# Behind the last head group: SiLU in one ACT instruction, the second output product by channel halves, normalisation pair by pair

## What is computed

```python
h = layer_norm(y, sb_norm_w, sb_norm_b) * (1.0 + scale) + shift
h = jax.nn.silu(h) @ out_w + out_b
return x + h
```

## Time and profile before

| what | value |
|---|---|
| median of 3 runs | 515.12 us (514.90 to 515.36) |
| time of the profiled execution | 515.57 us |
| its span, first to last instruction | 513.8 us |
| mean granted TensorE clock | 0.993 of full |
| PE busy | 504.3 us, 98% of the span |
| DVE / ACT / POOL busy | 412.0 / 344.6 / 220.4 us |

### The profile page before, as it was taken

One profiled execution on the slowest core, in us unless ns is written; L12 is line 12 of the kernel. 1 busy time (PEld: TensorE's weight loads), 2 busy tenths in 40 slices (PEclk: granted clock), 3 DMA queues, 4 the chain that ended last, 5 costly groups with the idle time before them and its releaser, 6 DMA issues.

```text
span 513.8 us, 9864 instructions
## 1 busy us (share of the span) xinstructions
PE 504.3 (98%) x3346; PEld 195.1 (38%) x3346; DVE 412.0 (80%) x1059; ACT 344.6 (67%) x677; POOL 220.4 (43%) x253
## 2 busy tenths in 40 slices
PE   9999899999999999999999999999999999999987
PEld 5563423333443244333433334332433333332234
DVE  4876897998897688966898688967899999999226
ACT  1453367776767675777768576777778778777961
POOL 3039749999143420832226430643672045005401
PEclk8899999999999999999999999999999999999999
DMA  6983232242214133110331133210331112211011
GB/s 240 349 273 102 80 93 79 64 143 83 76 53 125 41 124 125 41 43 17 113 122 43 43 97 110 68 49 11 124 124 43 43 43 87 81 44 43 2 41 42
DMA packets 43034, 45.26 MB, mean 88 GB/s; under 512 B 4436, under 2 KB 41572, under 8 KB 42600
## 3 DMA queue, kind: packets, MB, share of 16 engines
q1 hardware_dynamic: 42696, 42.79, 26.6%
q10 hardware_dynamic: 288, 1.84, 0.9%
HBM read 25.46 MB, written 18.87 MB: 86 GB/s over the span
## 4 chain that ended last, share of the span: by engine, by line
PE 75%; DVE 11%; issue 2%; POOL 2%; ACT 2%; POOLq 0%; DVEq 0%; ACTq 0%
PE bank L549 19%; PE bank L532 12%; PE bank L523 10%; PE bank L595 9%; PE bank L512 9%; DVE masked L862 7%; PE bank L623 4%; PE bank L606 4%; PE bank L564 2%; PE bank L584 2%; ACT probs L715 1%; DVE row_max L865 1%; PE bank L557 1%; PE bank L631 1%; POOL XN L836 1%
## 5 line engine op out<-in xcount | busy, mean ns | idle before, releaser
L715 ACT ACTIVATE probs<-bank 128x512 f32<-128x512 f32 x512 | 272.4, 600 | 82.0 <-PE bank L523 81.2
L865 DVE TENSOR_REDUCE row_max<-bank 128x1 f32<-128x512 f32 x256 | 162.9, 684 | 29.5 <-PE bank L532 27.9
L532 PE MATMUL bank<-k_s,q_s 64*128 64x512 f16 x512 | 182.7, 382 | 1.8 <-DVE row_max L865 1.2
L862 DVE CUSTOM_DVE_ANT_0 masked<-bank,mask_bias 128x512 bf16<-128x512 f32 x256 | 162.9, 687 | 13.0 <-PE bank L532 12.0
L512 PE MATMUL bank<-q_s,k_s 64*128 64x512 f16 x512 | 151.8, 381 | 0.9 <-ACT v_aug L783 0.5
L523 PE MATMUL bank<-shift,kx 64*128 64x512 f16 x512 | 148.6, 376 | 0.0
L549 PE MATMUL bank<-probs,v_aug 128*17 128x512 f32 x1024 | 135.4, 598 | 0.7 <-ACT probs L715 0.7
L532 PEld LDWEIGHTS bank<-k_s,q_s 64*128 64x128 f16 x512 | 46.1, 93 | 151.8 <-DVE row_max L862 67.1
L595 PE MATMUL bank<-xT,wqkv 128*128 128x512 f32 x128 | 61.7, 612 | 0.4 <-ACT xT L746 0.3
L523 PEld LDWEIGHTS bank<-shift,kx 64*128 64x128 f16 x512 | 46.8, 95 | 32.0
L512 PEld LDWEIGHTS bank<-q_s,k_s 64*128 64x128 f16 x512 | 31.6, 94 | 13.4 <-ACT probs L715 8.0
(11 more groups left out here) (111 smaller groups left out, 512.3 us busy)
## 6 DMA issues: line engine op xcount, KB each, us to landing
q_parts<-parts SPq DMA_DIRECT2D x64, 128.0 KB
k_parts<-parts SPq DMA_DIRECT2D x64, 128.0 KB
q_s<-q_parts SPq DMA_DIRECT2D x32, 256.0 KB, 2.7
k_s<-k_parts SPq DMA_DIRECT2D x32, 256.0 KB, 3.0
X<-in_x SPq DMA_DIRECT2D x4, 512.0 KB, 7.3
y<-X SPq DMA_DIRECT2D x7, 256.0 KB, 2.2
wc<-in_w_cond ACTq DMA_DIRECT2D x1, 1024.0 KB, 5.1
tables<-in_tables SPq DMA_DIRECT2D x4, 256.0 KB, 7.1
```

The lines of the kernel that those rows point to most:

```text
L532: nc.tensor.matmul(bank, m.q_s[slot][rows, i, queries], m.k_s[slot][rows, i, :], start=True, stop=True).then_inc(q.d_made, 1)
L715: act.activation(m.probs[k][:, h, :], bank, ACT.Exp, scale=1.0 if s >= B * NG else float(DH) ** -0.5)\
L862: dve.tensor_tensor_reduce(m.masked[D["max", n, k, h] % ND][:, :], bank, m.mask_bias[:, b, :], 1.0, LOWEST, ALU.add, ALU.max, to)\
L865: dve.tensor_reduce(to, bank, AX.X, ALU.max).then_inc(q.d_done, 1)
```

## The change

Four things change, all in the `last_batch` functions except where noted.

1. ACT applies SiLU itself: one instruction for each pair and half (L797 becomes an `ACT.Silu` that writes `xT`). DVE's eight instructions for halving and joining (L1045, L1050) go. Silu isn't in the set of functions that ACT has loaded, so a load of another table set is put behind the copies of `ACC`, along with an instruction on one column that nobody reads (`spare`). Scale and bias come unhalved from a small new tile `last_mod`, which POOL copies from `mod1` before it halves that (the exception).
2. DVE takes pair 0's normalisation before the last statistics of pair 1, not behind them.
3. PE turns pair 0, multiplies its channel half 0 with `out_w`, turns pair 1, and then goes on by halves: (pair 0, half 1), (pair 1, half 0), (pair 1, half 1). Each waits for one SiLU instruction.
4. `LAST_BUSY` goes from (14, 7) to (10, 4).

```diff
-LAST_BUSY = (14, 7)
-LAST_HALVED = [(0, 1), (0, 0), (1, 0), (1, 1)]
+LAST_BUSY = (10, 4)
...
+        m.last_mod = sb("last_mod", [P, 2, CT, 1])
...
         keep_busy(LAST_BUSY[0], m.d_banks[2])
-        for p in range(PAIRS):
-            for t in pair(p):
-                pe.wait_ge(q.last_normal, t + 1)
-                for h in range(CT):
-                    last = nc.tensor.transpose(m.a_banks[CT * p + h][:, t % 2 * P:(t % 2 + 1) * P],
-                                               last_normal(m)[:, t, h * P:(h + 1) * P], m.ident[:, :])
-            last.then_inc(q.last_tokens, 1)
+        last_turn(0)
         keep_busy(LAST_BUSY[1], m.d_banks[2])
-        for p in range(PAIRS):
-            pe.wait_ge(q.last_silu, CT * (p + 1))
-            for t in pair(p):
-                for k in range(CT):
-                    last = nc.tensor.matmul(sum_bank(m, t)[:, 0:C],
-                                            last_tokens(m)[:, k, t * P:(t + 1) * P], m.wo[1][:, k, :],
-                                            start=(k == 0), stop=(k == CT - 1))
+        last_products(0, 0)
+        last_turn(1)
+        last_products(0, 1)
+        last_products(1, 0)
+        last_products(1, 1)
+
+    def last_turn(p):
+        for t in pair(p):
+            pe.wait_ge(q.last_normal, t + 1)
+            for h in range(CT):
+                last = nc.tensor.transpose(m.a_banks[CT * p + h][:, t % 2 * P:(t % 2 + 1) * P],
+                                           last_normal(m)[:, t, h * P:(h + 1) * P], m.ident[:, :])
+        last.then_inc(q.last_tokens, 1)
+
+    def last_products(p, k):
+
+        pe.wait_ge(q.last_silu, CT * p + k + 1)
+        for t in pair(p):
+            last = nc.tensor.matmul(sum_bank(m, t)[:, 0:C], last_tokens(m)[:, k, t * P:(t + 1) * P], m.wo[1][:, k, :],
+                                    start=(k == 0), stop=(k == CT - 1))
+            if k == CT - 1:
                 last.then_inc(q.last_sum, 1)
...
-        act.wait_ge(q.silu_made, CT * LAST)
+
+        act.wait_ge(q.consts_made, SHIFTS)
+        act.activation(m.spare[:, :], m.ident[:, 0:1], ACT.Silu).then_inc(q.spare_made, 1)
+        act.wait_ge(q.mod1_step, 8)
+        await_read(act, q, len(USES) - 3)
         for p in range(PAIRS):
             act.wait_ge(q.last_tokens, p + 1)
             for h in range(CT):
-                if (p, h) == LAST_HALVED[0]:
-                    act.wait_ge(q.last_halved, 1)
-                act.activation(m.tanh[h][:, columns(p)], m.a_banks[CT * p + h][:, 0:2 * P], ACT.Tanh,
-                               bias=m.mod1[:, 1, h, LAST:B], scale=m.mod1[:, 0, h, LAST:B]).then_inc(q.last_tanh, 1)
+                act.activation(last_tokens(m)[:, h, columns(p)], m.a_banks[CT * p + h][:, 0:2 * P], ACT.Silu,
+                               bias=m.last_mod[:, 1, h, :], scale=m.last_mod[:, 0, h, :]).then_inc(q.last_silu, 1)
...
+        def moments(p):
+            await_steps()
             for t in pair(p):
                 dve.bn_aggr(m.last_moments[:, t, :], m.last_stats[:, t, :, :].rearrange("p n w -> p (n w)"))\
-                   .then_inc(q.last_step, 1)
-            steps_done += 2
-            dve.wait_ge(q.last_step, steps_done)
+                   .then_inc(q.last_moments, 1)
+            at = slice(2 * p, 2 * p + 2)
+            dve.wait_ge(q.last_moments, 2 * p + 2)
             dve.tensor_scalar(m.last_spread[:, at], m.last_moments[:, at, 1], 1e-5, None, ALU.add)\
                .then_inc(q.last_spread, 1)
+
+        def normal(p):
+            dve.wait_ge(q.last_rstd, p + 1)
+            for t in pair(p):
+                dve.tensor_scalar(last_normal(m)[:, t, :], O[:, t, :], m.last_moments[:, t, 0:1],
+                                  m.last_rstd[:, t:t + 1], ALU.subtract, ALU.mult).then_inc(q.last_normal, 1)
+
+        output_statistics(0)
+        moments(0)
+        output_statistics(1)
         await_turned(dve, q, NORMAL[-3])
...
+        normal(0)
+        moments(1)
+        normal(1)
...
         pool.wait_ge(q.mod1_step, 5)
+        pool.tensor_copy(m.last_mod[:, :, :, :], m.mod1[:, :, :, LAST:B]).then_inc(q.mod1_step, 1)
+        pool.wait_ge(q.mod1_step, 6)
```

More of the change, by code:

```diff
@@ L430, in build @@
         q.last_step = sem("last_step")
+        q.last_moments = sem("last_moments")
         q.last_spread = sem("last_spread")
@@ L434, in build @@
         q.last_tokens = sem("last_tokens")
-        q.last_halved = sem("last_halved")
-        q.last_tanh = sem("last_tanh")
+        q.spare_made = sem("spare_made")
         q.last_silu = sem("last_silu")
@@ L992, in halve @@
         bank = made(D[piece])
-        dve.wait_ge(q.mod1_step, 7)
+        dve.wait_ge(q.mod1_step, 8)
         dve.wait_ge(q.part_pool, 4 * (B - 1))
@@ L1007, in last_batch, with step, await_steps, output_statistics @@
         O = m.O[LAST % 2]
-        steps_done = TPB
-        for p in range(PAIRS):
+        steps = [TPB]
+        def step(ins):
+            ins.then_inc(q.last_step, 1)
+            steps[0] += 1
+        def await_steps():
+            dve.wait_ge(q.last_step, steps[0])
+        def output_statistics(p):
             at = slice(2 * p, 2 * p + 2)
@@ L1013, in last_batch @@
             dve.wait_ge(q.d_done, D["output", GROUPS - 2] + 1)
-            dve.reciprocal(m.inv_sum[:, at, :, :], bank[:, :, :, DH:DH + 1]).then_inc(q.last_step, 1)
-            steps_done += 1
-            dve.wait_ge(q.last_step, steps_done)
-            dve.tensor_tensor(O[:, at, EARLY:C].rearrange("p t (h d) -> p t h d", d=DH), bank[:, :, :, 0:DH],
-                              m.inv_sum[:, at, :, :].broadcast_to([P, 2, G, DH]), ALU.mult).then_inc(q.last_step, 1)
-            steps_done += 1
@@ L1020, in last_batch @@
-            dve.wait_ge(q.last_step, steps_done)
+            step(dve.reciprocal(m.inv_sum[:, at, :, :], bank[:, :, :, DH:DH + 1]))
+            await_steps()
+            step(dve.tensor_tensor(O[:, at, EARLY:C].rearrange("p t (h d) -> p t h d", d=DH), bank[:, :, :, 0:DH],
+                                   m.inv_sum[:, at, :, :].broadcast_to([P, 2, G, DH]), ALU.mult))
+            await_steps()
             for t in pair(p):
-                dve.bn_stats(m.last_stats[:, t, 1, :], O[:, t, EARLY:C]).then_inc(q.last_step, 1)
@@ L1023, in last_batch @@
-            steps_done += 2
-            dve.wait_ge(q.last_step, steps_done)
+                step(dve.bn_stats(m.last_stats[:, t, 1, :], O[:, t, EARLY:C]))
+        def moments(p):
+            await_steps()
             for t in pair(p):
                 dve.bn_aggr(m.last_moments[:, t, :], m.last_stats[:, t, :, :].rearrange("p n w -> p (n w)"))\
-                   .then_inc(q.last_step, 1)
-            steps_done += 2
-            dve.wait_ge(q.last_step, steps_done)
+                   .then_inc(q.last_moments, 1)
+            at = slice(2 * p, 2 * p + 2)
+            dve.wait_ge(q.last_moments, 2 * p + 2)
@@ L1030, in last_batch @@
             dve.tensor_scalar(m.last_spread[:, at], m.last_moments[:, at, 1], 1e-5, None, ALU.add)\
                .then_inc(q.last_spread, 1)
-        await_turned(dve, q, NORMAL[-3])
[L1033 to L1051, removed]
+        def normal(p):
[3 more added lines that the diff above has]
+                                  m.last_rstd[:, t:t + 1], ALU.subtract, ALU.mult).then_inc(q.last_normal, 1)
```

## The result

The changed kernel took 513.87 us (median of 12 runs, 513.65 to 514.54) against 515.21 us for the kernel before (12 runs, 514.90 to 515.56), a ratio of 0.9973 with a 95% interval of 0.9965 to 0.9981. That is 1.34 us less, where 1.4 had been forecast.

The account below looks back on a forecast made before the run. PE bounds the body, busy 98% of the span; the end is dense products behind a latency. Terms 0.42 + 1.55 - 0.56 = 1.41 us take the 515.12 us median to 513.7 us, range 513.2 to 514.6.

Parts of the forecast that it names:

- DVE's order: End, DVE: pair 0's `XN` starts at about 503.52 in place of 503.94, 0.42 us earlier.
- The sum: End: the forecast's terms for how much earlier the products end, 0.42 + 1.55 - 0.56 = 1.41 us.
- SiLU, 1.55 us: End, ACT: from ACT's start to the first product 0.70 us where it took 2.25, a gain of 1.55.
- The turn and the gap: End, PE: pair 1's turn between the products costs 0.46 us, the gap before pair 1 half 0 costs 0.10.
- Filler at no cost: End, PE: the four idle matmuls end at 505.45, out of the way by 0.10 us before the first product.
- Table load hidden: End, ACT: load and `spare` end at 502.4, hidden with 2.4 us to spare; without cover they cost 1.5 us.
- The rival's own sum: End, ACT: table load not hidden, priced at 2 us more than its room of 3.7 us, 514.3 us; chance 2%.
- Clock: End from 503.4 on, PE: rival that the clock falls, 517.9 us, chance 3%; forecast was that it stays at 1.00.
- the rival's mechanism: End, PE: with fewer idle matmuls the clock falls to 1.2 GHz, adding 4.2 us, 517.9 us in all; chance 3%.
- The body: Program before 500 us: not touched by the change; moving by more than 0.3 us would show the prediction wrong.
- my signs of being wrong: SiLU above 0.8 us, ACT's load past the turn, end's clock below 1, or body moved by more than 0.3 us.
- Writes: End, SP: last writes at a spacing of 0.43 us do not queue up; if they do, at most 0.4 us.

## Why the prediction was right

- **DVE's order, 0.42 us.** Right in kind: `XN` follows rstd by 0.11 (502.17 + 0.72 = 502.89, 503.00). Undone, it costs 0.35. But it is worth this only with pair 0's first half ahead of pair 1's turn; the term belongs to the two reorderings together, as does the 0.46 for the turn. The sum has it as a gain of its own, which it isn't. I had put `XN` 0.04 behind rstd; DVE's own statistics ended at 502.91, and it needed 0.09 behind those.
- **SiLU, 1.55 us.** SiLU over 256 tokens costs what the tanh did: 1.02 for two, so 0.56 and 0.46 on. From ACT's start to the first product it took 0.62 (504.35 to 504.97) where I had 0.70. From the copy to the first product it is 5.30 for 7.26 us, 1.96 less; the sum had 1.97. That these agree so closely is luck in part: DVE's order gave 0.07 less than forecast and SiLU 0.08 more.
- **The turn and the gap, 0.46 and 0.10 lost.** The turn holds PE for 0.44 (505.93 to 506.37). From the first product to the last residual sum's start it is now 4.25 us (504.97 to 509.22) where it was 3.67 (507.52 to 511.19): 0.58 lost, against 0.56. Here too the parts are not quite the forecast's: the gap ahead of pair 1's first half is 0.06, not 0.10, and pair 0's first half holds PE for 0.96 us (504.97 to 505.93), not 0.87. With fillers 14 and 7, where PE comes to it without a wait, that half takes 0.86 (505.76 to 506.62); what the other 0.10 is, no run shows.
- **Filler at no cost.** Right for 10 and 4 (with 10 and 0 the end is the same 9.55), and the step that mattered most without being a gain: with 14 and 7 it costs 0.56, and SiLU put into the kernel before with its 7 brings nothing.
- **Table load hidden.** Right, with 2.5 us between the end of `spare` (501.84) and SiLU (504.35). Exposed it costs 1.37, close to the 1.5 that I had put, as `spare` overlaps with the next instruction. The rival's own sum is wrong: a load that takes 2 us more than the 3.7 us of room would give 513.7 + 2 = 515.7 us, not 514.3.
- **Clock.** In the changed kernel it stays at 1.00, as forecast. My reason was that the new end is denser than a stretch that kept the clock: from 503 to 506 PE is busy for 2.53 us of 3. That reason fits, and no run tests it by itself. But I took the filler for dispensable in my expectation of the run without it, and there the rival's mechanism is real. Its price was 1.6 and 2.7 us at the two ends measured, since the clock came back before the products were through. The 4.2 that I had put isn't refuted by that: without any filler the profiled execution is the fastest of its kernel, and the slowest run, at 519.32 us, lies above the 517.9 of the rival.
- **The body.** One of my signs of being wrong did come up: the end starts 0.59 us earlier in the changed kernel's first profile than before, and I had allowed 0.3. It was a bad sign to choose, since executions of one kernel differ by as much (499.67 and 500.22). By itself the profiled pair would have shown 1.92 us (515.57 - 513.65); it takes the medians, or the end measured from the copy, to see the 1.4.
- **Writes.** The last residual sums are 0.43 apart, and from the last sum's start to the end of the span it is 2.7 us (511.9 - 509.22) where it was 2.6 (513.8 - 511.19), so the closer writes cost at most 0.1.

## What to carry to other kernels

At a program's end, walk the relay of waits with the durations of the trace; the gain is the earlier start of the last dense work less what is put between its pieces. Filler that keeps PE busy is a part of the schedule: it had to be shortened here when the wait that it covers got shorter, or it would have taken the gain away, and it couldn't be dropped from the long wait of 2.6 us, or the clock fell in the work behind it. A switch of ACT's tables was free here, with an instruction of the new set issued while ACT waited anyway. And where executions differ ahead of the place that was changed, compare that place from an anchor of its own.

## What the runs showed of the hardware that I had not expected

- With PE idle from about 501 to past 503, the granted clock fell to 0.50, but 2.7 us apart (counted from the copy) in two kernels with the same PE work until then, and it came back after some 3 us at 0.50 in one and some 7 in the other. The same program's opening shows 0.50 over different stretches in different executions, and its last stage starts up to 0.6 us apart; the second isn't explained by the first.
- An activation on 128 columns is issued 0.35 us behind the one before (four in 1.50), on 256 columns 0.46: half the columns take three quarters of the time.
